# Cross-attention of a post-norm decoder layer: values and sums of a head as one 64-column product

## The reference, cut to what matters

```python
NUM_HEADS = 16                       # so D = 32 channels a head
q = (query @ Wq + bq).reshape(B, Nq, H, D).transpose(0, 2, 1, 3)
k = (key_value @ Wk + bk).reshape(B, Nkv, H, D).transpose(0, 2, 1, 3)
v = (key_value @ Wv + bv).reshape(B, Nkv, H, D).transpose(0, 2, 1, 3)
attn = jnp.einsum('bhqd,bhkd->bhqk', q, k) * scale
attn = jnp.clip(attn, -CLAMP, CLAMP)
attn = jax.nn.softmax(attn, axis=-1)
x = jnp.einsum('bhqk,bhkd->bqhd', attn, v).reshape(B, Nq, Cq)
return x @ Wo + bo
```

## Time and profile before

| | |
|---|---|
| median of the runs shown | 3065.3 us (3062.53 to 3066.28, 3 runs) |
| the profiled execution, its own time | 3064.36 us |
| its span | 3062.6 us |
| PE / VectorE / ScalarE / GpSimd busy, share of the span | 87% / 80% / 49% / 5% |
| mean granted clock of TensorE | 0.905 of 2.4 GHz |
| matmuls of `values_of` (L1057) | 2048, 270.1 us busy |
| exponentials (L1393) | 256, 248.0 us busy |
| row maxima (L1887) | 256, 312.4 us busy |
| DMA | 332.84 MB in 197746 packets |

### The profile page before, as it was taken

How to read it: one execution, slowest core, us unless ns; L and a number is a source line. 1 busy time by engine, 2 the same in 40 slices (tenths; PEclk the granted TensorE clock), 3 DMA queues, 4 the chain that set the end, 5 groups by cost and what they waited for, 6 DMA issues and landing times.

```text
span 3062.6 us, 44241 instructions
## 1 busy us (share of the span) xinstructions
PE 2652.0 (87%) x13112; PEld 1025.9 (33%) x13160; DVE 2462.7 (80%) x4238; ACT 1495.8 (49%) x2424; POOL 159.1 (5%) x146
## 2 busy tenths in 40 slices
PE   7999989986777747777678889999999999999997
PEld 4544432221111104444334422222223444444443
DVE  5979869999988979999988588988888755455554
ACT  3320043335999989999822235555556322121121
POOL 0000033320000000000000000111100000000000
PEclk9999999995555559999988989999999999999999
DMA  8563122213333323333214453343455510000000
GB/s 314 180 237 137 62 103 104 96 83 107 124 120 120 124 92 118 111 110 117 69 57 134 165 118 102 106 112 97 115 158 184 205 69 28 28 28 28 28 28 28
DMA packets 197746, 332.84 MB, mean 109 GB/s; under 512 B 32505, under 2 KB 118521, under 8 KB 187249
## 3 DMA queue, kind: packets, MB, share of 16 engines
q1 hardware_dynamic: 193312, 314.51, 31.5%
q10 hardware_dynamic: 4304, 16.78, 1.4%
HBM read 200.70 MB, written 130.51 MB: 108 GB/s over the span
## 4 chain that ended last, share of the span: by engine, by line
PE 50%; issue 30%; DVE 15%; ACT 2%; DMA 1%; DVEq 1%; SPq 0%; ACTq 0%; POOLq 0%; POOL 0%
PE bank L1057 8%; PE bank L1224 7%; PE bank L1213 7%; DVE stats L1486 6%; PE bank L1013 4%; PE bank L1021 4%; PE bank L997 4%; PE bank L1111 3%; DVE arena L1785 2%; PE bank L834 1%; PE bank L841 1%; PE bank L1029 1%; ACT arena L1329 1%; PE bank L972 1%; PE bank L861 1%
## 5 line engine op out<-in xcount | busy, mean ns | idle before, releaser
L1486 DVE TENSOR_REDUCE stats<-bank 128x1024 f32 (+1 forms) x352 | 405.9, 1215 | 44.1 <-PE bank L898 26.8
L1311 ACT ACTIVATE arena<-arena,scale 128x512 bf16<-128x512 int8 x512 | 408.1, 802 | 54.3 <-DVE arena L1730 54.3
L921 PE MATMUL bank<-arena 64*128 64x512 bf16 x512 | 306.4, 605 | 105.7 <-DVE arena L1723 67.3
L1329 ACT ACTIVATE arena<-arena,scale 128x512 f32<-128x512 int8 x512 | 370.3, 802 | 13.3 <-DMA arena<-dq_scr 11.3
L1723 DVE CUSTOM_DVE_ANT_0 arena<-bank,arena,fac 128x512 int8<-128x512 f32 x512 | 349.5, 746 | 23.0 <-PE bank L921 10.3
L1887 DVE TENSOR_REDUCE arena<-bank 128x2 f32<-128x1024 f32 x256 | 312.4, 1223 | 55.6 <-PE bank L1013 39.9
L1393 ACT ACTIVATE arena<-bank 128x1024 f32<-128x1024 f32 x256 | 248.0, 1022 | 190.0 <-PE bank L1029 190.0
L1462 ACT ACTIVATE arena<-bank,bf_s,fac 128x512 f32<-128x512 f32 x128 | 99.5, 778 | 459.2 <-PE bank L1216 459.2
L1299 ACT ACTIVATE arena<-bank,floor_c,fac 128x1024 int8<-128x1024 f32 x96 | 115.5, 1204 | 341.3 <-PE bank L861 290.7
L1057 PE MATMUL bank<-arena 128*32 128x512 f32 x2048 | 270.1, 604 | 0.0
L2056 DVE TENSOR_SCALAR arena<-arena 128x512 f16<-128x512 f32 x128 | 54.6, 427 | 254.4 <-ACT arena L1462 254.4
(11 more groups left out here) (208 smaller groups left out, 3486.2 us busy)
## 6 DMA issues: line engine op xcount, KB each, us to landing
dq_scr<-arena SPq DMA_DIRECT2D x128, 256.0 KB, 2.0
arena<-dq_scr SPq DMA_DIRECT2D x128, 256.0 KB, 2.6
arena<-half_scr SPq DMA_DIRECT2D x256, 128.0 KB, 2.8
qkv_scr<-arena SPq DMA_DIRECT2D x8, 3072.0 KB, 9.7
arena<-in_x SPq DMA_DIRECT2D x16, 1024.0 KB, 8.1
half_scr<-arena SPq DMA_DIRECT2D x32, 512.0 KB, 3.9
arena<-qkv_scr SPq DMA_DIRECT2D x128, 128.0 KB, 2.3
x_scr<-arena SPq DMA_DIRECT2D x16, 1024.0 KB, 6.0
```

Source lines behind the costliest of these rows:

```text
L921: return mm(dst, qE[r, h // 2, P * t:P * t + P], kE[r, h // 2, :], start=True, stop=True)
L1311: last = A(e_dump[:, NT * (h % 2) + t, :], dq8[:, h % 4, t, :], ACT.Exp, bias=negm_b[:, par, c:c + 1], scale=scale[:, S_DOTS:S_DOTS + 1], ...
L1329: A(eG[:, s % 2, t, :], dqG[:, s % 4, t, :], ACT.Exp, bias=negm_g[:, par, c:c + 1], scale=scale[:, S_DOTS:S_DOTS + 1]).then_inc(S("eG_done ...
L1486: return V.tensor_reduce(dst, src, ax, ALU.max, apply_absolute_value=True)
```

## The change

The ones move into the values. `vX` has for every tile of keys and every head 64 columns in place of 32: 32 of values, loaded by the transfer, and 32 of ones, written once before the stage. One product of 64 columns then gives the values of a head on 32 partitions and its sum, repeated, on the next 32. Two heads lie side by side in a bank: in the first four steps heads 2 and 3 into bank 7, in the last four heads 0 and 1 into bank 6. So a step has two products in place of four, and the number of steps stays. Values and sums of a group are complete only when both banks are.

With that, `oX` holds two blocks of 512 (2 x 2 heads), `recB` too, and on every second strip of 32 partitions `oX` holds sums in place of values. `sumS` is gone. `recB` is set to zero once, and GpSimd's multiply covers 1024 elements. `store_group` is four transfers, the load of `vX` writes runs of 32 floats with gaps of 32, `store_sums` waits for both copies and moves a group later, and with it `load_spread`, `invert`, `store_rec`, `load_rec` and `store_group`. The copy of bank 7 must now wait for a free place in `oX` as the copy of bank 6 does. For the last two groups VectorE moves the sums beside the values with copies before it inverts them.

```diff
-        vX = cX(F32, 2, NT, P)
+        vX = cX(F32, 2, NT * G, 2 * XD)
-        oX = cX(F32, 4, T)
-        sumS = cX(F32, 2, T)
-        recB = cX(F32, 2, T)
+        oX = cX(F32, 4, 2, T)
+        recB = cX(F32, 2, 2, T)
+        sum_tail = eT[:, 0, 1, 0:2, :]
...
-                sp.dma_start(vX[:, par], at4(v_scr, i)).then_inc(S(f"vX_in{par}"), 16)
+                src = v_scr[i].rearrange("p t n -> p (t n)") if isinstance(i, int) else v_scr[bass.ds(i, 1)].rearrange("a p t n -> p (a t n)")
+                sp.dma_start(vX[:, par, :, 0:XD], src.rearrange("p (q x) -> p q x", x=XD)).then_inc(S(f"vX_in{par}"), 16)
...
-                sp.dma_start(dst, oX[:, r]).then_inc(S(f"oX_stored{r % 2}"), 16)
+                for g in range(G):
+                    q = 2 * XD * (g % 2)
+                    sp.dma_start(dst[XD * g:XD * g + XD, :], oX[q:q + XD, r, g // 2, :]).then_inc(S(f"oX_stored{r % 2}"), 16)
...
-            def store_sums(i, par):
+            def store_sums(i, r):
                 sp.wait_ge(S("sumS_done"), i + 1)
+                sp.wait_ge(S("oX_evac"), i + 1)
                 hold(sp)
-                sp.dma_start(group_of(sums_scr, i), sumS[0:P:XD, par, :]).then_inc(S(f"sums_stored{par}"), 16)
+                dst = group_of(sums_scr, i).rearrange("(n a) t -> a n t", a=2)
+                sp.dma_start(dst, oX[XD:P:2 * XD, r, :, :]).then_inc(S(f"sums_stored{r % 2}"), 16)
...
-                if not (known and i < 2):
-                    store_rec(i - 2)
+                if not (known and i < 3):
+                    store_rec(i - 3)
+                if not (known and i < 4):
+                    store_group(i - 4, r)
+                if not (known and i < 2):
+                    store_sums(i - 2, (r + 2) % 4)
                 if not (known and i < 3):
-                    store_group(i - 3, (r + 1) % 4)
-                if not (known and i < 1) and not (known and i == GROUPS - 1):
-                    store_sums(i - 1, (r + 1) % 2)
+                    load_rec(i - 3, (r + 1) % 2)
                 if not (known and i < 2):
-                    load_rec(i - 2, r % 2)
-                if not (known and i < 1) and not (known and i == GROUPS - 1):
-                    load_spread(i - 1, (r + 1) % 2)
+                    load_spread(i - 2, r % 2)
...
-                nc.gpsimd.tensor_tensor(oX[:, r, :], oX[:, r, :], recB[:, par, :], ALU.mult).then_inc(S("oX_ready"), 1)
+                flat = lambda a: a.rearrange("p n t -> p (n t)")
+                nc.gpsimd.tensor_tensor(flat(oX[:, r]), flat(oX[:, r]), flat(recB[:, par]), ALU.mult).then_inc(S("oX_ready"), 1)
...
-                if k == 2 and half == 0:
                     pe.wait_ge(S(f"vX_in{par}"), i * 8 + 16 - 8 * par)
-                    if not (isinstance(i, int) and i == 0):
-                        pe.wait_ge(S("oX_evac"), i)
+                if k == 2 and half == 0 and not (isinstance(i, int) and i == 0):
+                    pe.wait_ge(S("oX_evac"), i)
                 hold(pe)
-                for g in range(G):
-                    w = ones if k < 2 else vX[:, par, c, XD * g:XD * g + XD]
-                    last = mm(bank[XD * g:XD * g + XD, 7 if k < 2 else 6, :], w, eT[:, par, g, c, :],
+                for g in ((2, 3) if k < 2 else (0, 1)):
+                    q = 2 * XD * (g % 2)
+                    last = mm(bank[q:q + 2 * XD, 7 if k < 2 else 6, :], vX[:, par, c * G + g, :], eT[:, par, g, c, :],
                               start=c == 0, stop=c == NT - 1)
...
-            def sums_out(i, par):
+            def free_place(i, r):
+                if not (isinstance(i, int) and i < 4):
+                    act.wait_ge(S(f"oX_stored{r % 2}"), ((i - 2) * 8 - 8 * (r % 2)) * G)
+
+            def sums_out(i, r):
...
-                A(sumS[:, par], bank[:, 7, :], ACT.Copy).then_inc(S("sumS_done"), 1)
+                A(oX[:, r, 1, :], bank[:, 7, :], ACT.Copy).then_inc(S("sumS_done"), 1)
...
-            link(V.memset(ones, 1.0))
+            link(V.memset(vX.rearrange("p a q x -> p (a q) x")[:, :, XD:2 * XD], 1.0))
+            link(V.memset(recB.rearrange("p a n t -> p (a n t)"), 0.0))
...
-                link(V.reciprocal(sumS[:, i % 2, :], sumS[:, i % 2, :]))
                 dve.wait_ge(S("oX_evac"), i + 1)
+                dve.wait_ge(S("pvX_mm"), GROUPS)
                 dve.wait_ge(S("oX_ready"), i)
-                V.tensor_tensor(oX[:, i % 4, :], oX[:, i % 4, :], sumS[:, i % 2, :], ALU.mult).then_inc(S("oX_ready"), 1)
+                for q in (0, 2 * XD):
+                    link(V.tensor_copy(sum_tail[q:q + XD], oX[q + XD:q + 2 * XD, i % 4]))
+                link(V.reciprocal(sum_tail[0:3 * XD], sum_tail[0:3 * XD]))
+                V.tensor_tensor(oX[0:3 * XD, i % 4], oX[0:3 * XD, i % 4], sum_tail[0:3 * XD], ALU.mult
+                                ).then_inc(S("oX_ready"), 1)
```

More of the change, by code:

```diff
@@ L101, in sem @@
             return ctx.enter_context(nc.semaphore(name))
-        ARENA = 190 * 1024 // 4
+        ARENA = 197 * 1024 // 4
         arena = sb("arena", [P, ARENA], F32)
@@ L360, in decoder @@
         nmT = cX(BF16, 2, T)
-        ones = cX(F32, XD)
         ones_b = cX(BF16, P)
@@ L390, in decoder @@
         bfull_p = cW(F32, D)
-        assert cX.at <= cW.at
+        cW.at = max(cW.at, cX.at)
         arep_f = cW(F32, D)
@@ L644, in load_rec @@
                     row = rec_scr[i, g:g + 1, :] if isinstance(i, int) else rec_scr[bass.ds(i, 1), g, :]
-                    sp.dma_start(recB[XD * g:XD * g + XD, par, :], row.broadcast_to([XD, T])).then_inc(S(f"rec_in{par}"), 16)
+                    q = 2 * XD * (g % 2)
+                    sp.dma_start(recB[q:q + XD, par, g // 2, :], row.broadcast_to([XD, T])).then_inc(S(f"rec_in{par}"), 16)
             def load_values(b, par):
@@ L690, in _ @@
                 group_dma(i, i % 4)
-            for i in (GROUPS - 3, GROUPS - 2, GROUPS - 1):
+            store_rec(GROUPS - 3)
+            load_rec(GROUPS - 3, (GROUPS - 3) % 2)
+            for i in range(GROUPS - 4, GROUPS):
                 store_group(i, i % 4)
             for par in (0, 1):
-                sp.wait_ge(S(f"oX_stored{par}"), 8 * GROUPS)
+                sp.wait_ge(S(f"oX_stored{par}"), 4 * 8 * GROUPS)
             def store_x2(b, par):
@@ L1362, in _ @@
             barrier(act, 9)
-            def sums_out(i, par):
+            def free_place(i, r):
+                if not (isinstance(i, int) and i < 4):
+                    act.wait_ge(S(f"oX_stored{r % 2}"), ((i - 2) * 8 - 8 * (r % 2)) * G)
+            def sums_out(i, r):
                 act.wait_ge(S("sumX_mm"), i + 1)
-                if not (isinstance(i, int) and i < 2):
-                    act.wait_ge(S(f"sums_stored{par}"), i * 8 - 8 * par)
-                A(sumS[:, par], bank[:, 7, :], ACT.Copy).then_inc(S("sumS_done"), 1)
+                free_place(i, r)
+                A(oX[:, r, 1, :], bank[:, 7, :], ACT.Copy).then_inc(S("sumS_done"), 1)
             def values_out(i, r):
                 act.wait_ge(S("pvX_mm"), i + 1)
-                if not (isinstance(i, int) and i < 4):
-                    act.wait_ge(S(f"oX_stored{r % 2}"), (i - 2) * 8 - 8 * (r % 2))
-                A(oX[:, r, :], bank[:, 6, :], ACT.Copy).then_inc(S("oX_evac"), 1)
+                free_place(i, r)
+                A(oX[:, r, 0, :], bank[:, 6, :], ACT.Copy).then_inc(S("oX_evac"), 1)
             def max_turned(i, par):
@@ L1387, in group @@
                     if c == 2 and not (isinstance(i, int) and i == 0):
-                        sums_out(i - 1, (r + 1) % 2)
+                        sums_out(i - 1, (r + 3) % 4)
                     if c == NT - 1 and not (isinstance(i, int) and i == GROUPS - 1):
@@ L1403, in _ @@
             values_out(GROUPS - 2, 2)
-            sums_out(GROUPS - 1, 1)
+            sums_out(GROUPS - 1, 3)
             values_out(GROUPS - 1, 3)
@@ L1433, in _ @@
             for par in (0, 1):
-                act.wait_ge(S(f"oX_stored{par}"), 8 * GROUPS)
+                act.wait_ge(S(f"oX_stored{par}"), 4 * 8 * GROUPS)
             widen_weight(wnh)
@@ L1945, in group @@
                             clip(i, r, 2, None)
-                        if (c, u) == (3, 1) and not (isinstance(i, int) and i < 2):
+                        if (c, u) == (3, 1) and not (isinstance(i, int) and i < 3):
+                            invert(i - 3)
+                        if (c, u) == (3, 1) and last:
                             invert(i - 2)
@@ L1952, in _ @@
                     max_pair(h, h // G, h % G, u, START_AT[h * 2 + u])
-            group(0, 0)
-            group(1, 1)
-            with dve.Fori(1, GROUPS // 2 - 1) as j:
+            for i in range(4):
+                group(i, i % 2)
+            with dve.Fori(2, GROUPS // 2 - 1) as j:
                 for r in range(2):
```

## The result

The changed kernel takes 3131.3 us (median; 3130.22 to 3135.66), the kernel before 3065.3 in the same session: **slower, 1.0219 times [1.0202, 1.0237]**, 66 us. The profiled execution is the longest of its four, 3135.66 us, with a span of 3133.7: 71.1 above the span before.

| | us |
|---|---|
| up to the fifth group of the cross-attention | 2.9 |
| 25 groups, 1848.98 to 2337.22 (488.24 in place of 436.33) | 51.9 |
| of these, VectorE held by GpSimd's multiply (39.6, before 1.7) | 37.9 |
| of these, longer steps, 25 x 0.075 | 1.9 |
| of these, the rest | 12.1 |

The account below looks back on a forecast made before the run. TensorE was taken as full, with VectorE close behind. From 3064.4 us, -4 (steps) + 42 (GpSimd's multiply holding VectorE) + 4 (stage's end) gave 3106, or 3107 as median; range 3079 to 3150.

Parts of the forecast that it names:

- The main step: In the cross-attention groups, GpSimd's doubled multiply holds VectorE's arena instructions: 1.5 us x 28 = 42 us lost.
- the steps: TensorE's product steps in cross-attention: 0.97 us each, 0.03 less than before, a gain of 4 us over 31 groups.
- the end: Stage's end: longer VectorE divisions of the last two groups and a later load for batch 2, 4 us lost.
- (a): Cross-attention groups: GpSimd's multiply holds VectorE, the forecast itself; bounds 0.6 and 2.4 us a group, 3079 to 3136; chance 0.77.
- rival d: Cross-attention steps: the two 64-column products do not overlap, 220 us more, 3280 and up; chance 0.03.
- The start of the multiply: GpSimd's multiply in each group: starts 3.1 us later with a 2.95 us issue price, 0.6 without; the first was taken.
- L1903, due at 2036.98, would wait: VectorE in a group: with GpSimd running from 2036.1 to 2038.5, this instruction waits 1.5 us, 1.2 to 1.5 reaching TensorE.
- the other case that I had placed: VectorE in a group: a multiply starting between the two priced times, from 2034.5 say, holds L1898 for 1.8 us.
- rival (b): Cross-attention groups: multiply starts between 2035.7 and 2036.5, L1903 to L1905 not held, not slower: 3064 or 3060; chance 0.10.
- the wait before the sixth unit: Projection behind the stage: VectorE's divisions and five additions end at 2359.7, where TensorE wants its sixth unit at 2354.7.
- Rival (c): ScalarE's copy of sums waits for a place in oX: 1 to 2 us a group more, 3140 to 3170; chance 0.10.
- my sign, "over 3 us": ScalarE's copy of the sums: the forecast is wrong if this copy waits over 3 us.

Follow-up runs that it names:

- tiny_pool: The changed kernel, but GpSimd multiplies 4 elements of a partition in place of 1024, leaving out the division: 3077.4 us, 1.0042.
- before_pool1024: The kernel before, with only GpSimd's multiply doubled from 512 to 1024 elements, the added half zeros: 3090.0 us, 1.0085.
- v_one_run: The changed kernel, with v loaded in one 2 KB run a partition in place of 16 of 128 bytes; products read wrong places: 3102.1 us, 1.0116.
- tail_invert: The changed kernel, with VectorE's extra reciprocal of group 29 after the two last clips in place of before them: 3136.6 us, 1.0234.
- gated_end: The changed kernel, multiply in two halves waiting for VectorE gaps, second sums buffer, reciprocal stores before group stores, group 30's division beside the last products: 3076.3 us, 1.0037.
- Split_pool: The changed kernel, with GpSimd's multiply as two of 512 elements, one right behind the other: 3124.2 us, 1.0195.

## Why the prediction was right, and where it was off

**Right: the sign, the cause, the order of size.** 3107 was forecast, 3131 measured, inside 3079 to 3150. The main step, a doubled multiply that no longer fits the gap between two of DVE's arena instructions, is shown by tiny_pool (54 us gone with it) and by before_pool1024 (25 us come with it alone). Its price was given as 42 us. In the 25 groups DVE was held 37.9 us more than before, and 5.9 us more in the last groups, of which 2.8 at most came through to PE ahead of its wait and 1.9 lie in that wait.

**In part luck.** That 42 and 38 lie so near is partly luck: the multiply started 1.4 us earlier in the group than I took, and what it held was L1898's successor, not L1903's. I also took the whole overlap of two instructions for the loss, 0.15 us too much each time (before_pool1024). The sum is 24 us short, by the steps (6 us, with the wrong sign), the clock (12) and the end (9), less the 4 us that the price of the hold was too high. 3131 lies inside the bounds of (a) only because these allowed 2.4 us a group for a hold that was 1.6; a group was forecast at 18.7 us and is 19.5.

**The step of the products: mis-sized, with the wrong sign.** "I take 0.97 us a step" measured 1.01, and the 4 us gained became 2.3 lost. The overlap of the two products was right (rival d is out). What was wrong was to carry over the 0.02 us between four starts as overhead of an instruction. Of the longer step I can only show the weight loads: at full clock 134 ns for L1064 (tiny_pool), 108 before; whether they make the 0.01 us is open.

**The start of the multiply: between my bounds.** I set 0.6 us later without a price for the issue behind the load of v and 3.1 with it, and took the second. It was 1.7 (14.06 against 12.36): the issue took 1.3 to 1.55 us in these groups, 0.9 to 1.6 in all, not 2.95. So "L1903, due at 2036.98, would wait" was wrong, and the other case that I had placed, "it holds L1898 for 1.8", is what happens: 1.75 us in the group shown, 1.3 on average for L1908 alone. v_one_run shows that this start is worth 29 us, the clock included.

**Whom the multiply holds.** I had priced L1903, with its two inputs, as held like L1898, and rival (b) needed it free. On these rows 16 elements with one input are held in either form, TENSOR_SCALAR (L1908) and CAST (L1910: 2.23 us at 1877.28 in v_one_run, 0.20 alone), and so are two inputs (L1913, 1.38 us in tail_invert). Reciprocal and reduction from the bank are not. The reciprocal at 2395.00 in the changed kernel starts 0.11 us into a multiply and takes its 0.25 us, while the clip behind it takes 2.6 in place of 0.7. In gated_end a reciprocal of 6.55 us (from 2337.49) and four multiplies of 1.26 us (from 2341.13) run side by side, and neither is longer. No reduction took over 1.23 us in the changed kernel. Rival (b) is therefore out by both its conditions: the multiply did not start in its window, and two inputs are held. The Trainium skill (SBUF — State Buffer, "SBUF: two separate sides") lets DVE take the shared ports with two SBUF inputs or in its two-port modes, and blocks the loser for the whole instruction; the trace agrees, with these 1.38 us for the two inputs that no row of before showed.

**Missed: the clock.** 12 to 13 us, in no term of the sum. It is 12.1 as what is left in the 25 groups, and nearly the same from two like groups. A group with 3.4 us at half clock is 19.81 us long with L1908 at 0.93 us (from 2062.55); in v_one_run a group with L1908 at 0.94 and clock 1.00 is 18.22. The difference, 1.59, times the 27.3 / 3.41 = 8 such stretches is 12.7. I had taken PE's stop as its only price. In the 25 groups of the changed kernel the clock fell behind 8 of 15 stops of 1.66 to 2.07 us, and behind none of the 10 of 0.6 to 1.5. It stayed up behind those of 0.7 to 1.4 in before_pool1024 and v_one_run, and behind the one of 1.96 in v_one_run. Split_pool, with stops of 1.4 to 2.0 in most groups, spent 6.8 us at half clock where the changed kernel spent 27.3. What makes one stop bring a fall and another not is open, and no run has the same stops with the clock up, so the size is an estimate.

**The end: 4 us forecast, about 13 measured.** PE's waits are 7.5 + 4.2 + 0.2 + 0.6 less the 2.4 of before = 10.1; another 3.1 us went as its last products ran at half clock behind the first of these waits. My two divisions of 9.4 us and the wait before the sixth unit were right in place (forecast 5.0, measured 4.21). The 7.5 us ahead of them I did not see: I had costed the moved `load_spread` and `invert` at nothing, in the loop and in the last group alike. In the loop there is a group's time for the round through memory; in the last group two rounds follow each other behind one buffer, and the last clips stand behind them.

**Rival (c)** had 0.10: ScalarE's copy of the sums waited for oX's stores once in the whole stage, 3.9 us at 2352.41, and PE lost 0.64 us by it. That was behind an issue of 9.38 us (`store_rec` at 2339.78), with the projection's first loads just ahead of it on the queue. As a cost of each group it is out; my sign, "over 3 us", did not say whether once or in each group.

**Is there a version that wins?** Not on these numbers. The new products are not shorter (1.01 against 1.00 us), so with most of POOL's price taken away and part of the end's, 3076 is still above 3065.

## What to carry to other kernels

Before you lengthen an instruction on GpSimd, list the gaps between VectorE's instructions that it holds (here those on the arena alone, the reciprocal excepted), and then work out in which of them it will start: both its length and every issue ahead of its input on the queue decide that. Fewer, wider matrix products are no gain where the streaming is the same; here half the instructions took 1.01 us in place of 1.00, of which 0.86 is the streaming. When a chain of stores and loads is moved a group back, price the last group by itself: two rounds through one buffer stand there in a row, and taking out the first wait gives the time back only if the next one in the chain goes too.

## What the runs showed of the hardware that I had not expected

- Two multiplies of 1.27 us, one right behind the other, are no two chances for VectorE: one 16-element instruction got in between, and the next took 1.19 us in place of 0.175.
- The issue behind a load of 128 x 16 runs of 128 bytes took 0.9 to 1.6 us, behind the same bytes in 128 runs 0.38.
- Eight of 15 stops of TensorE of 1.66 to 2.07 us, once in 19 to 20 us, were followed by 3.4 us at 1.2 GHz, in a stretch where the clock had been 2.4 GHz throughout.
- A reciprocal of 6.55 us on VectorE and four multiplies of 1.26 us on GpSimd ran side by side, all of them on the arena, and none took longer than alone.
